# Ranked expert slots (128 up to 240 rows), high weights applied to both halves of the rows in one matmul, and a trimmed attention stage

## The reference

```python
# attention over 20000 edges, sorted by dst; 8 heads of 64
h = layer_norm(node_feature, ln1_g, ln1_b)
qkv = (h @ Wqkv + bqkv).reshape(N, 3, H, DH)
logits = jnp.einsum('ehd,ehd->eh', q[src], k[dst])
a = logits + dist_attn + path_attn        # softmax over the edges of one dst
msg = v[src] * sa[:, :, None]             # summed per dst, then @ Wo + bo
h2 = jax.nn.gelu(h2 @ W1 + b1, approximate=False) @ W2 + b2
...
# experts: top 2 of 8, hidden 1024, and one shared expert
shared = jax.nn.silu(xt @ sw1) * (xt @ sw3) @ sw2
_, idx = jax.lax.top_k(scores + biases, K)
h = jax.nn.silu(jnp.einsum('td,edh->eth', xt, w1)) * jnp.einsum('td,edh->eth', xt, w3)
y = jnp.einsum('eth,ehd->etd', h, w2)
out = jnp.einsum('te,etd->td', comb, y) + shared
```

## Time and profile before

| | |
|---|---|
| executions | median 868.16 us (867.26 to 869.63, n=3) |
| profiled execution | 868.55 us, its span 866.9 us |
| mean granted TensorE clock | 0.962 |
| PE busy | 793.6 us (92%), 5533 matmuls |
| DVE busy | 547.8 us (63%), 938 instructions |
| ACT busy | 439.5 us (51%), 685 instructions |
| POOL busy | 183.7 us (21%), 156 instructions |
| attention, 100.95 to 318.7 us | PE 4.8 to 5.2 us per block |
| experts, 562.17 to 834.45 us | PE without a gap in the chain |

### The profile page before, as it was taken

How to read it: one execution, slowest core, us unless ns; L and a number is a source line. 1 busy time by engine, 2 the same in 40 slices (tenths; PEclk the granted TensorE clock), 3 DMA queues, 4 the chain that set the end, 5 groups by cost and what they waited for, 6 DMA issues and landing times. The chain is left out here.

```text
span 866.9 us, 14506 instructions
## 1 busy us (share of the span) xinstructions
PE 793.6 (92%) x5533; PEld 676.0 (78%) x5533; DVE 547.8 (63%) x938; ACT 439.5 (51%) x685; POOL 183.7 (21%) x156
## 2 busy tenths in 40 slices
PE   3996899999999978799997899799999999999993
PEld 2653677787777764699996799699999999999992
DVE  6537998989898935444225544466666666675635
ACT  4244686868686843634342442244545445445420
POOL 9140654545554530000000004000000000000022
PEclk9999899999999989799999799889999999999997
DMA  8320900000000007000002914276756757745024
GB/s 274 100 46 6 365 22 2 1 2 1 2 2 1 2 1 255 0 1 1 1 1 79 388 45 160 78 234 197 237 187 221 249 186 231 228 163 162 22 64 140
DMA packets 64105, 94.39 MB, mean 109 GB/s; under 512 B 6483, under 2 KB 39861, under 8 KB 63525
## 3 DMA queue, kind: packets, MB, share of 16 engines
q1 hardware_dynamic: 61797, 87.74, 30.6%
q0 software_dynamic: 2240, 5.76, 2.2%
HBM read 81.35 MB, written 12.13 MB: 108 GB/s over the span
## 5 line engine op out<-in xcount | busy, mean ns | idle before, releaser
L658 DVE TENSOR_SCALAR onehot<-iota_n,records 128x640 fp32r<-128x640 f32 x160 | 137.0, 879 | 4.0 <-PE ps L776 4.0
L1536 DVE TENSOR_TENSOR w_lo<-weights_far,w_hi 128x1024 fp32r<-128x1024 f32 x64 | 78.3, 1225 | 33.8 <-ACT w_hi L1627 33.8
L1639 ACT ACTIVATE hT<-ps 128x224 f32<-128x224 f32 x64 | 22.9, 358 | 129.9 <-PE ps L1706 129.9
L643 POOL TENSOR_TENSOR bias_exp_hi<-edge_exp_hi,mask 128x640 fp32r<-128x640 f32 x40 | 60.8, 1519 | 119.3 <-DVE mask L663 94.0
L1706 PE MATMUL ps<-xT_hi,w_hi 128*128 128x224 f32 x512 | 79.1, 277 | 3.5 <-DVE w_lo L1536 3.5
L1706 PE MATMUL ps<-xT_lo,w_hi 128*128 128x224 f32 x512 | 79.0, 277 | 0.0
L1706 PE MATMUL ps<-xT_hi,w_lo 128*128 128x224 f32 x512 | 78.8, 276 | 0.0
L1706 PEld LDWEIGHTS ps<-xT_hi,w_hi 128*128 128x128 f32 x512 | 70.9, 195 | 7.0 <-issue 3.8
L776 PE MATMUL ps<-onehot,bias_exp_hi 128*128 128x320 f32 x400 | 70.0, 322 | 6.8 <-DVE onehot L658 6.8
L1522 POOL DMA_INDIRECT weights_far<-slot_results,gate x5 | 4.8, 959 | 303.4 <-DMA slot_results<-weights_near 302.2
L1706 PEld LDWEIGHTS ps<-xT_lo,w_hi 128*128 128x128 f32 x512 | 68.6, 195 | 0.0
(11 more groups left out here) (261 smaller groups left out, 1674.6 us busy)
## 6 DMA issues: line engine op xcount, KB each, us to landing
weights_far<-in_L_ffn_w SPq DMA_DIRECT2D x56, 512.0 KB, 5.6
weights_near<-in_L_ffn_w SPq DMA_DIRECT2D x28, 512.0 KB, 3.6
weights_near<-in_L_gnn_W SPq DMA_DIRECT2D x1, 4096.0 KB, 14.6
weights_far<-in_L_ffn_w SPq DMA_DIRECT2D x2, 2048.0 KB, 19.8
slot_rows<-zeros SPq DMA_DIRECT2D x1, 3584.0 KB, 23.2
vs<-slot_rows SPq DMA_DIRECT2D x8, 448.0 KB, 6.9
slot_results<-weights_near SPq DMA_DIRECT2D x16, 224.0 KB, 5.9
weights_near<-in_L_gnn_Wqkv SPq DMA_DIRECT2D x3, 1024.0 KB, 7.7
```

The costliest lines, as they stand in the source:

```text
L643: pool.tensor_tensor(to.rearrange("p t (h d) -> p t h d", h=H), e[:, b, :, :].unsqueeze(3).broadcast_to([P, CT, H, BN]), m.unsqueeze(2).br ...
L658: dve.tensor_scalar(onehot[b % 2][:, t, :], iota_n[:, :], rec[:, b, t, 0:1], None, ALU.is_equal).then_inc(oh_ready, 1)
L1536: dve.tensor_tensor(to[1], frm, to[0], ALU.subtract).then_inc(w_lo_ready, 1)
L1639: act.activation(gated[m][:, 0:CAP], psum[2 * m][:, 0:CAP], ACT.Silu).then_inc(a_sb, 1)
```

## The change

1. **Slots by rank.** DVE ranks the experts by count in routing (`rank`, `order`). Rank 0 is the emptiest. The capacity of rank r is 128 + 16r (`CAPS`, 128 to 240), 1472 slots in all. SP reads the expert's number from `most` when it loads the weights. Rank 0's weights are loaded only when the order is known, in 12 transfers of 512 KB. If any expert has more rows than its rank's capacity, the general stage runs.
2. **Both parts in one matmul.** `x_hi` and `x_lo` lie beside each other. A w_hi matmul moves both (2·cap columns, the x_lo result at column 240 of the bank); a w_lo matmul moves x_hi alone. So 8 matmuls for 12. ACT then copies the x_lo halves of both banks to SBUF (`low_part`), DVE adds the other halves (`parts_summed`), ACT's Silu reads and writes that sum (`gate`), and `hidden` multiplies two SBUF tiles. Rank 0 has one row block in `turn` and `down`, the others two (128 and the rest).
3. **POOL subtracts w2.** The third `weights_lo` of each unit is POOL's, with a semaphore of its own.
4. **Attention.** 628 columns for 640; the one-hot rows of tiles 0 and 1 in one instruction; masks for 8 blocks at once, made after the collection of a group; for the first two blocks PE waits per tile; POOL waits for the one-hot rows of block b-1 before it starts block b.
5. **Blocks.** The special and the general stage share one `Block` each, for attention and for the experts. All loops over experts are written out.
6. **End.** DVE makes the scaled additions of tiles 0 and 1 between its last shared-expert steps and those of 2 to 4 before all five final additions.

```diff
-BLK = 112
-CAP = CB * BLK
+CAP = 240
+STEP = 16
+CAPS = [CAP - STEP * (EX - 1 - r) for r in range(EX)]
+def slot_blocks(r):
+    return [(s, min(P, CAPS[r] - s)) for s in range(0, CAPS[r], P)]
...
-            for to, frm in expert_parts(slots, 3, w1[0], w3[0], w2[0]):
-                sp.dma_start(to, frm).then_inc(w_in[0], 16)
             sp.wait_ge(slots_ready, 1)
             fullest = sp.value_load(most[0:1, 0:1], min_val=0, max_val=NP)
             with sp.If(fullest < CAP + 1):
+                load_expert(sp, most, 0, (w1, w3, w2), routed_slots(slots), raw_in)
                 sp.wait_ge(scattered, 16 * 2 * NT)
...
+    e = sp.snap(sp.value_load(most[0:1, 1 + r:2 + r], min_val=0, max_val=EX - 1))
...
@@ POOL, experts @@
+            for v in range(V + 1):
+                u = v % UNITS
+                pool.wait_ge(w_hi_ready, 3 * v + 3)
+                pool.tensor_tensor(w2s[u][1], raw_rest[2] if v == V else raw[u][2], w2s[u][0], ALU.subtract)\
+                    .then_inc(w2_lo_ready, 1)
...
@@ DVE, experts @@
+            def parts_summed(v, m):
+                cap = CAPS[v // UNITS]
+                dve.wait_ge(a_low, v * UM + m + 1)
+                dve.tensor_tensor(pair(v, m), pair(v, m), banks[:, 2 * m:2 * m + 2, 0:cap], ALU.add).then_inc(a_sum, 1)
+            def hidden(v, m):
+                dve.wait_ge(a_sb, v * UM + m + 1)
+                dve.tensor_tensor(unit_hidden(h32_all, v)[:, m, :], pair(v, m)[:, 0, :], pair(v, m)[:, 1, :], ALU.mult)
...
+            for v in range(V):
+                r, u = v // UNITS, v % UNITS
+                weights_lo(v + 1, 0)
+                parts_summed(v, 0)
+                weights_lo(v + 1, 1)
+                hidden(v, 0)
+                if u == 1 and r:
+                    results(r - 1)
+                parts_summed(v, 1)
+                if u == 2 and r + 1 < EX:
+                    rows_lo(r + 1)
+                hidden(v, 1)
+                low_hidden(v)
...
@@ ACT, experts @@
+            def low_part(v, m):
+                act.wait_ge(a_ps, v * UM + m + 1)
+                act.activation(pair(v, m), banks[:, 2 * m:2 * m + 2, CAP:CAP + cap], ACT.Copy).then_inc(a_low, 1)
+            def gate(v, m):
+                act.wait_ge(a_sum, v * UM + m + 1)
+                act.activation(pair(v, m)[:, 0, :], pair(v, m)[:, 0, :], ACT.Silu).then_inc(a_sb, 1)
...
@@ PE, experts @@
-                                    last = pe.matmul(psum[2 * m + n][:, 0:CAP], w[u % 2][wp][:, c, m * P:(m + 1) * P],
+                        for c in range(DC):
+                            pe.matmul(both(bank, cap), w[u % 2][0][:, c, cut], xT(r)[:, c, :, :], start=c == 0, stop=False)
+                        for c in range(DC):
+                            last = pe.matmul(bank[:, 0:cap], w[u % 2][1][:, c, cut], xT(r)[:, c, 0, :], start=False,
...
@@ POOL, attention @@
-                    pool.wait_ge(masked, b + 1)
+                pool.wait_ge(masked, b // BPT + 1)
+                if b:
+                    pool.wait_ge(oh_ready, (CT - 1) * b)
```

More of the change, by code:

```diff
@@ L31 @@
 EX = 8
+SRC = 2 * (-(-N // 4) * 2)
+SH = SRC // 2
 NT = -(-N // P)
@@ new lines, in weighted_sums @@
+            def weighted_sums(j):
+                pe.wait_ge(pt_ready, BPT * (j + 1))
+                for pair in range(H // 2):
+                    for t in range(NT):
+                        for odd in range(2):
+                            h, r = 2 * pair + odd, slice(DH * odd, DH * (odd + 1))
+                            n = P if t < NT - 1 else LAST
+                            last = pe.matmul(psO[r, pair * P:(pair + 1) * P], vs[0:n, t, h * DH:(h + 1) * DH],
+                                             PT[0:n, t, h, :], start=t == 0, stop=t == NT - 1)
+                last.then_inc(o_ready, 1)
@@ L822, in feed_forward @@
+            for b in range(NB):
+                sums(b, 0)
+                if b % BPT == 1 and b > 1:
+                    weighted_sums(b // BPT - 1)
+                sums(b, 1)
+                logits(b)
+                if b:
+                    turn(b - 1)
+            turn(NB - 1)
+            weighted_sums(NT - 1)
 def feed_forward(nc, sem, finished, x, W2, rows_b, rows_c, wo, w_near, w_far, xs, hT, vs, work, small, ident, psum):
@@ L1080, in routing_units @@
     weighed = work[:, D + 740:D + 780].rearrange("p (t e) -> p t e", t=NT)
+    key, rank, behind, order = (work[:, D + 784 + 8 * i:D + 792 + 8 * i] for i in range(4))
+    among, owner = (work[:, D + 816 + EX * EX * i:D + 816 + EX * EX * (i + 1)].rearrange("p (a b) -> p a b", a=EX)
+                    for i in range(2))
     eps = small[:, 0:1]
@@ L1780, in experts_all @@
+def experts_all(nc, block, sem, w_in, w1, w3, w2, sw1, sw3, sw2, out, slots, big, xs, hT, work, gate_sb, most, psum):
     gates = gate_views(gate_sb)["gates"]
@@ new lines, in _, with expert @@
+    @block.scalar
+    def _(act):
+        fullest = act.value_load(most[0:1, 0:1], min_val=0, max_val=NP)
+        with act.If(fullest > CAP):
+            def expert(e, chunks=HC):
+                for i in range(2 * chunks):
+                    wait_past(act, a_ps, e * (2 * HC) + (i + 1))
+                    wait_past(act, b_sb, e * (2 * HC) + (i - 1))
+                    act.activation(gated[i % 2], psum[2 * (i % 2)][:, 0:HALF], ACT.Silu).then_inc(a_sb, 1)
+            for k in range(2):
+                expert(k)
+            with act.Fori(1, EX // 2) as j:
+                for k in range(2):
+                    expert(j * 2 + k)
+            expert(EX, UM)
```

1568 lines of the change are left out of this document (766 added, 802 removed).

## The result

The changed kernel takes 862.28 us (median, 861.25 to 863.21, n=4); the kernel before took 868.36 on the same chip. The ratio is 0.9929, 95% interval 0.9911 to 0.9947: faster by 6 us, where 35 were forecast and the range ended at 844. The profiled execution has a span of 860.5 us, 6.4 less than before.

A forecast was written before the change was run, and what follows sets the result against it. PE was taken to bound the experts, DVE or PE attention's blocks. Terms −18.5 (experts), −12 (attention), −0.5, −0.9, −1.5, −0.7 and −1 summed to −35.1 from 868.2: 833.5 us, range 818 to 844.

The forecast's parts named there:

- The step that failed: Experts: DVE's results and rows_lo fall into the time it waits for POOL and cost nothing.
- the hold: Experts: POOL's w2 subtraction, first by 0.3 us, makes DVE's second hidden wait; 2.4 us, bounds 2.04 to 2.6.
- The half sentence behind it: Experts: without POOL holding DVE, results and rows_lo are some 0.7 us each on a path with 2 us of slack.
- The clock rival: Experts: TensorE's clock falls in PE's pauses; kernel 870 us and more; clock or counts 0.05, of which 0.04 slower.
- the last one: Sign against the prediction: a granted TensorE clock under 1.00 after 570 us.
- ACT's turn: Experts: ACT's time per unit, POOL's 2.4 us included, bounds ranks 0 to 6; 7.7 us at cap 184, PE's 7.28.
- The estimate by the Trainium skill, GPSIMD Engine Reference, section 3.1: Experts: POOL's subtraction takes 2.25 us, half of 4.5 for 2048 elements; the sum would be 3.5 us lower.
- PE's line: PE matmuls: columns / 2.4 plus 18 ns each, least 110 ns; units by rank 5.15 to 8.16 us.
- the rival without a hold: Experts: DVE and POOL run side by side, or DVE comes first; PE bounds each rank, 821 us; chance 0.22.
- Attention: Attention's 38 blocks: mean 5.09 to 4.77 us, PE bounding, DVE's turn 4.55; −12 us.
- The smaller terms: Outside attention blocks and experts: first sums −0.5, Blocks −0.9 and −1.5, experts' start −0.7, final additions −1 us; routing's additions hidden.
- The tail: End: DVE's scaled additions come ahead of the last sums, POOL's last gather binds, end 858.3 instead of 859.24; −1 us.

The follow-up runs named there:

- e2: Changed kernel with w2's subtraction moved from POOL back to DVE, after low_hidden, and results still late: 844.28 us, ratio 0.9724.
- e1: Changed kernel with DVE's results copy moved to the first unit of a rank, before hidden(v,1): 836.88 us, ratio 0.9633.
- e5: Changed kernel with ten matmuls, results thrown away, before the down that waits for results at each change of rank: 854.31 us, ratio 0.9835.
- e8: Changed kernel with results back at its place before the change, behind the first w_lo of a rank's second unit: 845.91 us, ratio 0.973.
- e4: Changed kernel with results early, in a rank's first unit, and ACT's split of w2 after its second gate: 848.1 us, ratio 0.9765.
- e3: Changed kernel with both results early, in a rank's first unit, and w2's subtraction on DVE: 826.83 us, ratio 0.9522.
- e6: Kernel with early results and w2's subtraction on DVE, all ranks given 240 slots: 857.95 us, ratio 0.9866.
- e9: Changed kernel with early results and w2's subtraction halved, one piece of 512 on POOL, the other on DVE: 828.46 us, ratio 0.9524.

## Why the prediction was wrong

**The step that failed** is one sentence of the experts' part: "results and rows_lo of DVE fall into the hold and cost nothing". rows_lo does: it stands ahead of hidden(v,1). results stands elsewhere in the list, after hidden(v,0) of the second unit, and so behind the hold of the unit before, low_hidden, two w_lo of 1.2 us, a sum and `hidden`. PE's first `down` of a rank waits for it, 18.9 us in seven changes of rank, and the stage grew by 4.0 us where 18.5 less were forecast. I had costed results by its duration, 0.7 us, and had not asked when it comes and who waits for it. The half sentence behind it, that without the hold the copy has 2 us of slack, failed too: in e2, without the hold but with w2's subtraction on DVE, PE waited 12.3 us for it. Moving this one copy brought 25 us (e1), to 836.88, within the range of the record.

**The clock rival** was seen and priced, but at the wrong place. I looked at the pauses of rank 0, forecast at 2 us a unit; the trace has about 1 us each, and they left the clock alone. The pauses that the failed step made, 2.2 to 5.0 us, did lower it. e5, in which results comes no sooner, shows 8 us of the loss to be this. The prediction's evidence, a fall after a pause of 3.41 us and none in the window from 325, was no bound: here the clock fell after 2.2, and in e8 once after 1.68. Of the signs that were to show the prediction wrong, the last one came: a granted clock under 1.00 after 570 us.

**What was right.** The hold: its direction (POOL first, by 0.43 us where 0.3 was worked out), its length (2.40 us, as taken), and ACT's turn: by rank 7.16, 7.25, 7.4, 7.5, 7.6, 7.7, 7.9 and 8.05 us for 7.28, 7.40, 7.51, 7.63, 7.75, 7.87, 7.98 and 8.16 worked out. This is the rule of the Trainium skill, SBUF — State Buffer, "Who interferes with whom": who issues first has the shared ports for the whole instruction. The traces agree in both orders: POOL first at `hidden` and in e4 at low_hidden, DVE first in attention. The estimate by the Trainium skill, GPSIMD Engine Reference, section 3.1, 2.25 us, was 0.15 short of the 2.40 measured. PE's line: e3's units from rank 1 on lie within 0.2 us of it, e6's within 0.13, and e6 gave 31 us for 33.

**Readings of the prediction that do not hold.** The 2.03 us of two one-hots beside POOL were taken as a sign for the rival without a hold, since only 1.0 us was lost. The row merges one of 0.55 and one of 1.57 us, and the line's own durations show it (ns min/median/max):

```profile
L658 DVE TENSOR_SCALAR onehot<-iota_n,records x160: 532/688/1577, 86.5 to 306.6; 128x640 fp32r<-128x640 f32 x160
```

The second one-hot started 0.3 us behind POOL's product (206.64 to 208.16) and ended 0.35 us after it. So the trace of before already had DVE waiting for POOL, and spoke against that rival. Two smaller slips: the line columns / 2.4 + 18 ns gives 151 ns for 320 columns where 146.5 were read, so it fits two of its three points; and a hold of 2.25 us in place of 2.4 makes the forecast's terms 4.2 us smaller (seven ranks of four units), not 3.5.

**Attention** was mis-sized by 3 us, one each for three things: the first block took 5.87 us, the four with the weighted sums 9.54 (9.57 before; 9.3 by the forecast), and the others 4.80 for 4.77. **The smaller terms**: routing took 1.5 us more for its extra DVE instructions and the later weights, which I had priced at nothing with 2 us as the bound; how these two share it was not tried. The tail gave nothing: the ten gathers now start every 1.45 us on the average (832.92 to 846.01) for 1.33 (838.29 to 850.28), and the last rows bound the end. That DVE's scaled additions beside them are the cause is possible and was not tried.

Taking the two together: the changed kernel loses 25 us to a copy's place beside the hold (16 of it to the move; some 8 of the whole through the clock), and 10 more to the hold once the copy is early. Without both it is 826.83, 42 us faster than before.

## What to carry to other kernels

A small instruction is to be costed by its place: list what stands ahead of it in its engine's queue and who waits for it, above all where a loop is written out anew and a line moves by two or three places. When work goes to POOL, look at which DVE instructions on SBUF tiles run beside it (here those with two tensor inputs, and the one-hots with one), and which is released first; a hold is harmless only while the turn that contains it stays under the bounding engine's. A saved microsecond on the bounding engine shows only if no new pause opens there, and a pause can cost twice, as here, once itself and once in the clock after it.

## What the runs showed of the hardware

TensorE's granted clock fell after single pauses of 2.2 to 2.9 us between stretches of full work (0.66 in the windows at 630 and 665 us of the changed kernel) and stayed at 1.00 after those of 1.9 and 2.0 us. The length of the pause alone does not decide: in e8 the clock fell after one of 1.68 us, and in e5 it stayed at 1.00 after one of 2.73 us that had ten matmuls ahead of it. In e8, after one of 3.35 us, the first three matmuls still ran at full speed (0.23 us apart) and the next eight at the lower level (0.43). Filling the pauses with matmuls whose results are thrown away was worth more than it cost, 8 us net in e5.

POOL's subtraction of 1024 elements took 2.36 to 2.65 us wherever it started ahead of DVE (the changed kernel, e1 and e4), and one of 512 elements 1.30 us (e9, median). Only the second to come showed the wait in its duration: DVE's `hidden` 2.12 us for 0.30, its low_hidden 2.4 for 0.5 in e4, POOL's product 2.54 for 1.52 behind DVE's pair of one-hots. A one-hot with one tensor input waited as well: 1.57 us behind POOL's product, 0.53 with POOL idle.
